# Adding expert results straight into the output, with 71 expert tiles and a rearranged routing stage

## What is computed

```python
h = rmsnorm(layernorm(x), ln1_w)              # then q, k, v, rotary, causal attention, wo
x2 = layernorm(x) + attn @ wo.T
h = rmsnorm(x2, ln2_w).reshape(4096, 256)
topw, topi = top_k(softmax(h @ gate_w.T), 2)  # 8 experts, 2 for each token
topw = topw / topw.sum(-1)
for e in range(8):
    g = silu(h @ w1[e].T) * (h @ w3[e].T)     # 512 wide
    out += (g @ w2[e].T) * wfull[:, e:e + 1]  # 0 where e is not chosen
return x + x2 + out
```

## Time and profile before

| | |
|---|---|
| median of 3 runs | 2072.73 us (2072.46 to 2073.15) |
| the profiled execution | 2073.89 us, span 2072.1 us |
| TensorE busy | 1817.0 us (88%) |
| VectorE busy | 1227.2 us (59%) |
| ScalarE busy | 990.4 us (48%) |
| GpSimd busy | 504.0 us (24%) |
| stage 7 | 1460 to 1616 us |
| stage 8 | 1616 to 2053 us |
| stage 9 | to 2072 us |

### The profile page before, as it was taken

One profiled execution on the slowest core, in us unless ns is written; L12 is line 12 of the kernel. 1 busy time (PEld: TensorE's weight loads), 2 busy tenths in 40 slices (PEclk: granted clock), 3 DMA queues, 4 the chain that ended last, 5 costly groups with the idle time before them and its releaser, 6 DMA issues. The chain is left out here.

```text
span 2072.1 us, 33460 instructions
## 1 busy us (share of the span) xinstructions
PE 1817.0 (88%) x10357; PEld 958.4 (46%) x10358; DVE 1227.2 (59%) x3167; ACT 990.4 (48%) x2129; POOL 504.0 (24%) x740
## 2 busy tenths in 40 slices
PE   5795779884899999999999999999875799999994
PEld 5622656552333333333333333332665466666662
DVE  2388236886888888787888888782466122222220
ACT  2201115431477776767777776867643122222221
POOL 2100302366302030210203030000387122333331
PEclk9997899985899999999999999999986899999997
DMA  4000000000000000000000000000356222222223
GB/s 134 0 0 0 1 1 1 4 18 0 1 2 2 1 2 2 2 1 2 2 2 2 2 2 2 2 1 1 114 170 220 57 47 47 47 47 47 45 47 97
DMA packets 55929, 60.83 MB, mean 29 GB/s; under 512 B 11533, under 2 KB 51638, under 8 KB 55734
## 3 DMA queue, kind: packets, MB, share of 16 engines
q1 hardware_dynamic: 33712, 33.86, 5.5%
q0 software_dynamic: 13440, 18.36, 5.2%
q10 hardware_dynamic: 8646, 6.96, 1.0%
HBM read 34.82 MB, written 28.12 MB: 30 GB/s over the span
## 5 line engine op out<-in xcount | busy, mean ns | idle before, releaser
L1452 ACT ACTIVATE prob<-pS 128x512 f32<-128x512 f32 (+3 forms) x1280 | 600.3, 536 | 245.9 <-PE pS L1366 126.3
L1495 DVE TENSOR_REDUCE mx<-pM 128x1 f32<-128x512 f32 x768 | 501.2, 685 | 92.6 <-PE pM L1346 89.4
L1346 PE MATMUL pM<-KT,QT 96*128 96x512 bf16 (+3 forms) x1280 | 440.9, 356 | 11.7 <-ACT QT L1434 7.3
L1362 PE MATMUL pS<-QT,KT 99*128 99x512 bf16 (+3 forms) x1280 | 416.5, 350 | 14.5 <-ACT prob L1452 9.1
L1381 PE MATMUL pO<-prob,VV 128*32 128x512 f32 (+3 forms) x2560 | 300.6, 542 | 14.2 <-ACT prob L1452 14.0
L1491 DVE CUSTOM_DVE_ANT_0 junk<-pM,mask_row 128x128 bf16<-128x128 f32 (+3 forms) x512 | 243.6, 485 | 71.9 <-PE pM L1346 70.7
L2115 PE MATMUL pH<-w13T,QKV 128*128 x576 | 260.6, 595 | 1.7 <-ACT QKV L2161 1.7
L1346 PEld LDWEIGHTS pM<-KT,QT 96*128 96x128 bf16 x1280 | 124.0, 98 | 263.3 <-DVE mx L1495 99.6
L2203 DVE COPY QKV<-pG 128x512 f32<-128x512 f32 x72 | 49.8, 692 | 317.1 <-PE pG L2124 317.1
L1362 PEld LDWEIGHTS pS<-QT,KT 99*128 99x128 bf16 x1280 | 123.6, 98 | 148.8 <-ACT prob L1452 81.8
L1289 POOL CAST mpart<-mneg 128x16 bf16<-128x16 f32 x32 | 6.8, 213 | 749.6 <-DVE mneg L1503 749.6
(11 more groups left out here) (312 smaller groups left out, 2374.9 us busy)
## 6 DMA issues: line engine op xcount, KB each, us to landing
raw<-in_ffn_w_dram SPq DMA_DIRECT2D x48, 256.0 KB
QKV<-queue SPq DMA_DIRECT2D x72, 136.0 KB, 2.1
x<-_attn_hidden_states_dram SPq DMA_DIRECT2D x32, 128.0 KB, 2.2
acc<-x ACTq DMA_DIRECT2D x8, 512.0 KB
QT<-mrow SPq DMA_DIRECT2D x128, 3.0 KB
queue<-pad_rec SPq DMA_DIRECT2D x9, 136.0 KB
acc<-QKV POOLq DMA_INDIRECT x72
wc_s<-in_attn_Wc_dram ACTq DMA_DIRECT2D x1, 1024.0 KB
```

Of the source, the lines that this page charges most:

```text
L1346: last = nc.tensor.matmul(pM[:, bank, 0:w], QT[0:ROWS, par, h, qt * P:(qt + 1) * P], KT[0:ROWS, par, 512 * part:512 * part + w], start=Tru ...
L1362: last = nc.tensor.matmul(pS[:, p % NSC, lo:512], KT[0:ROWS + 3, par, kt * P:(kt + 1) * P], QT[0:ROWS + 3, par, h, 512 * c + lo:512 * c + ...
L1452: nc.scalar.activation(prob[:, n % 3, h, lo:512], pS[:, p % NSC, lo:512], ACT.Exp, scale=SCALE).then_inc(s.head_exp, 1)
L1495: nc.vector.reduce_max(mx[:, h, qt, part:part + 1], pM[:, plan.bank[item], 0:w], AX.X).then_inc(s.unit_max, 1)
```

## The change

1. Stage 9 and `acc` go. The residual rows are written to the output itself in stage 7, and stage 8's puts add into the output.
2. The output has no rows behind its last token, so padding rows name real tokens, and hold zeros. Two rows of one put may not name the same token. Among the first 128 tokens, a token that is not expert e's is taken for the padding of e: one-hot matrices on VectorE (`spare_hot`, beat 2) and eight small matmuls on TensorE (`spare_tokens`, beat 3) list them; an expert with 128 tokens or more names tokens 0 to 127 in order. ScalarE zeroes a tile of 8 x 272 columns in beat 9.
3. `MAXT` is 71.
4. The eight padding writes are shared by SyncE (even experts) and ScalarE (odd ones). The zero tile at the queue's end is written in beat 2.
5. The residual sum goes from GpSimd to VectorE, at the end of a beat. The first norm's reciprocal roots and negative means are made for all 32 tiles at once by GpSimd in stage 6, after k = 2; `root1` and `negative_mean` go.
6. GpSimd takes `root2` between its two halves of scatters. ScalarE takes the exponential after `h_out` and the first quarter of `weights_out`.
7. Weight block 18 and the ones after it change PSUM banks, because one bank holds the spare tokens for a while.

```diff
-MAXT = 2 * B * L // P + E
+MAXT = 2 * B * L // P + E - 1
@@ stage6, GpSimd
+                def residual_norm():
+                    eps, rstd, shift = (v.norm1[:, n, :] for n in range(3))
+                    nc.gpsimd.tensor_scalar(eps, v.mv5[:, :, 1], 1e-5, None, ALU.add).then_inc(s.norm1, 1)
+                    nc.gpsimd.tensor_scalar(shift, v.mv5[:, :, 0], -1.0, None, ALU.mult).then_inc(s.norm1, 1)
+                    pool.wait_ge(s.norm1, 2)
+                    nc.gpsimd.tensor_tensor(rstd, eps, u.halfpow[:, :].to_broadcast([P, T]), ALU.pow).then_inc(s.norm1, 1)
+                    pool.wait_ge(s.norm1, 3)
+                    nc.gpsimd.tensor_tensor(shift, shift, rstd, ALU.mult).then_inc(s.norm1, 1)
+                    pool.wait_ge(s.norm1, 4)
...
+                    if k == 2:
+                        residual_norm()
@@ stage7, SyncE
                 for beat in range(LATE):
+                    if beat == 2:
+                        sp.wait_ge(s.pad_in, 1)
+                        sp.dma_start(v.queue[E * CAP:E * CAP + P, :], pad).then_inc(s.trash_in, 16)
                     for n in weights_in(beat):
                         raw_load(n)
-                sp.wait_ge(s.pads_known, 1)
-                for e in range(E):
+                sp.wait_ge(s.pads_known, 2)
+                for e in range(0, E, 2):
                     row = sp.value_load(v.pad_at[0:1, e:e + 1], min_val=0, max_val=E * CAP)
-                    sp.dma_start(v.queue[bass.ds(row, P), :], pad[:, :]).then_inc(s.padded, 16)
+                    sp.dma_start(v.queue[bass.ds(row, P), :], padr[:, e, :]).then_inc(s.padded, 16)
@@ GpSimd
                 for beat in range(1, LATE):
                     if beat >= 3:
                         scatter(beat - 3, 0, 4)
-                    if beat + 1 < NQ:
-                        root1(beat + 1)
+                    if beat <= NQ:
+                        root2(beat - 1)
                     if beat >= 3:
                         scatter(beat - 3, 4, 4)
-                    if beat <= NQ:
-                        root2(beat - 1)
-                        residual(beat - 1)
@@ TensorE
+                def spare_tokens():
+                    pe.wait_ge(s.pad_hot, E)
+                    pe.wait_ge(s.wT_out, CUT - RP + 1)
+                    for e in range(E):
+                        last = nc.tensor.matmul(pW[:, CUT % RP, e:e + 1], spare[:, e, :], self_f[:, :], start=True, stop=True)
+                    last.then_inc(s.pad_mm, 1)
@@ ScalarE
+                    if beat == NQ + 1:
+                        act.wait_ge(s.proj, T)
+                        act.wait_ge(s.logits, T // 2)
+                        nc.scalar.activation(turned[:, :], ones[:, 0:1].to_broadcast([P, E * REC]), ACT.Copy,
+                                             scale=0.0).then_inc(s.pad_zero, 1)
                     for j in range(2):
                         if beat < NQ:
                             attended_out(2 * beat + j)
-                        if j == 0 and 2 <= beat <= NQ + 1:
-                            exponential(beat - 2)
                         if 1 <= beat <= NQ:
                             h_out(2 * (beat - 1) + j)
                         weights_out(ws[j * quarter:(j + 1) * quarter])
+                        if j == 0 and 2 <= beat <= NQ + 1:
+                            exponential(beat - 2)
...
+                act.wait_ge(s.pads_known, 2)
+                for e in range(1, E, 2):
+                    row = act.value_load(v.pad_at[0:1, e:e + 1], min_val=0, max_val=E * CAP)
+                    act.dma_start(v.queue[bass.ds(row, P), :], padr[:, e, :]).then_inc(s.padded, 16)
@@ VectorE
+                def residual(q):
+                    four = slice(G * q, G * q + G)
+                    dve.wait_ge(s.x2, G * q + G)
+                    nc.vector.tensor_tensor(x1[:, four, :], x1[:, four, :], QKV[:, four, 0:H], ALU.add).then_inc(s.resid, 1)
...
+                def spare_hot():
...
+                    for e in range(E):
+                        nc.vector.tensor_scalar(spare[:, e, :], column, absent[:, 1, e:e + 1], absent[:, 0, e:e + 1],
+                                                ALU.is_equal, ALU.mult).then_inc(s.pad_hot, 1)
...
                     if 2 <= beat <= NQ + 1:
                         settle(beat - 2)
+                    if beat == 2:
+                        spare_hot()
+                    if beat < NQ:
+                        residual(beat)
@@ stage8
-                with eng.Fori(0, MAXT // R - 1) as i:
+                with eng.Fori(0, (LAST - 2) // R) as i:
...
-                            out=v.acc[:, :], out_offset=bass.IndirectOffsetOnAxis(ap=tail[:, k, E:E + 1], axis=0),
+                            out=v.out_rows[:, :], out_offset=bass.IndirectOffsetOnAxis(ap=tail[:, k, E:E + 1], axis=0),
@@ stage9
-            sp.dma_start(out_rows, acc_rows).then_inc(put, 16)
-            sp.wait_ge(put, 16)
```

More of the change, by code:

```diff
@@ L856, in stages_layer2 @@
         mv5 = sb("mv5", [P, T, 2], F32, late)
+        norm1 = sb("norm1", [P, 3, T], F32, late)
         jrow_i = sb("jrow_i", [P, NTAB], I32, late)
@@ L863, in stages_layer2 @@
         queue = nc.dram_tensor("queue", [E * CAP + P, REC], F32).ap()
-        acc = nc.dram_tensor("acc", [B * L + P, H], F32).ap()
+        out_rows = v.out.rearrange("b l h -> (b l) h")
         with ExitStack() as att:
@@ L1565, in stage7 @@
         junk = sb("junk7", [P, 2, H], BF16, ctx)
-        aT = sb("aT7", [P, 2, 2, C, P], F32, ctx)
-        hT = sb("hT7", [P, 2, 2, C, P], F32, ctx)
+        turned = sb("turned7", [P, E * REC], F32, ctx)
+        aT, hT = (turned[:, 4 * C * P * n:4 * C * P * (n + 1)].rearrange("p (i j c n) -> p i j c n", i=2, j=2, c=C)
+                  for n in range(2))
+        padr = turned[:, :].rearrange("p (e w) -> p e w", e=E)
         ln2c = sb("ln2c", [P, C], F32, ctx)
@@ L1574, in stage7 @@
         iota8 = sb("iota8", [P, E], F32, ctx)
+        self_i = sb("self_i7", [P, 1], I32, ctx)
+        self_f = sb("self_f7", [P, 1], F32, ctx)
+        absent = sb("absent7", [P, 3, E], F32, ctx)
+        early = w2T[:, :, :].rearrange("p f n -> p (f n)")
+        spare = early[:, 0:E * P].rearrange("p (e n) -> p e n", e=E)
+        column = early[:, E * P:E * P + P]
+        pad = early[:, E * P + 2 * P:E * P + 2 * P + REC]
+        column_i = early[:, E * P + P:E * P + 2 * P].bitcast(I32)
         cmp = xl[:, :, :].rearrange("p g h -> p (g h)")[:, 0:E * NTAB].rearrange("p (e j) -> p e j", e=E)
@@ L1792, in _ @@
                     turn_weights(ws[3 * quarter:])
+                    if beat == 3:
+                        spare_tokens()
             @block.scalar
             def _(act):
-                acc_rows = v.acc[0:B * L, :].rearrange("(t p) h -> p t h", p=P)
+                token_rows = v.out_rows.rearrange("(t p) h -> p t h", p=P)
                 def attended_out(i):
@@ L1962, in _ @@
                                             ALU.mult).then_inc(s.gw_ready, 1)
-                negative_mean(0)
-                negative_mean(1)
                 for beat in range(LATE):
@@ L1969, in _ @@
                         choose(beat - 2)
+                    if beat == 4:
+                        spare_out()
                     if beat < NQ:
                         attended(beat)
-                    if 1 <= beat and beat + 1 < NQ:
-                        negative_mean(beat + 1)
                     if 2 <= beat <= NQ + 1:
                         settle(beat - 2)
+                    if beat == 2:
+                        spare_hot()
+                    if beat < NQ:
+                        residual(beat)
                 dve.wait_ge(s.total, 1)
@@ L2072, in _ @@
                             load(R * i + k + R, k)
+                    for j in range(MAXT // R * R, MAXT):
+                        sp.wait_ge(s.x_T, j - R + 1)
+                        sp.wait_ge(s.tail_in, j - R + 1)
+                        load(j, j % R)
                 @block.gpsimd
@@ L2095, in _ @@
                             keep(k, i + 1)
-                    for j in range(MAXT - R + 1, MAXT):
+                    for j in range(MAXT // R * R - R + 1, MAXT):
                         put(j, j % R)
+                        if j + R - 1 >= MAXT // R * R and j + R - 1 < MAXT:
+                            keep((j + R - 1) % R, (j + R - 1) // R)
                     pool.wait_ge(y_put, 16 * MAXT)
@@ L2212, in _ @@
                     steps(dve, step)
-def stage9(nc, sb, ps, sem, env, base_env):
-    v, u = Names(env), base_env
-    put = sem("f_put")
-    with nc.Block() as block:
-        @block.sync
-        def _(sp):
-            out_rows = u.out.rearrange("b l h -> (b l h)").rearrange("(a n) -> a n", a=P)
-            acc_rows = v.acc[0:B * L, :].rearrange("l h -> (l h)").rearrange("(a n) -> a n", a=P)
-            sp.dma_start(out_rows, acc_rows).then_inc(put, 16)
-            sp.wait_ge(put, 16)
```

93 lines of the change are left out of this document (48 added, 45 removed).

## The result

The changed kernel took 2035.02 us (median, 2034.13 to 2035.73); the kernel before, timed beside it, 2072.6 (2069.19 to 2073.15). The ratio is 0.982, with an interval of 0.981 to 0.984: 33 to 40 us faster. The forecast was 2027.6, 7.4 us too fast. Its direction and its range (2016 to 2042) held; the narrower stretch of 2022 to 2034, to which it gave most weight, did not, nor did the size of the gain: 45.1 us were forecast, 37.6 lie between the medians.

What follows compares the result with a forecast made beforehand. GpSimd was taken to bound stage 7's beats 3 to 7, SyncE's padding its end, TensorE the expert tiles. Copy 18.0, tile 5.8 and stage 7 21.3 sum to 45.1 us off 2072.73: 2027.6, range 2016 to 2042.

Steps and rivals of the forecast that it cites:

- That closing: End of the kernel, after the last put's landing: closing the block was taken as 1.0 us, making the copy's gain 18.0.
- what is late next is this pair: End of stage 7: padding and scatters end together, so stage 8 starts at 1595 instead of 1616.3, gaining 21.3 us.
- Last scatter's end 1593.0: Stage 7, GpSimd: 1608.1 - 19.8 - 2.1 + 1.2 + 2.6 + 3.0 = 1593.0 us.
- The wait for squares: Stage 7: root2, between the scatter halves, waits once on GpSimd for ScalarE's squares, about 2.6 us.
- The stalls beside the residual: Stage 7: VectorE's residual stalls GpSimd six times, 0.2 us each, costing 1.2 (0 to 7).
- The "remote" waits: Stage 7: VectorE's waits for something on none of its engines reach GpSimd more, costing 3 us (0 to 8).
- rival 3: Stage 7, the port: each VectorE residual stops a scatter for 1.2 us and delays root2; 6 us more, 2033; chance 0.05.
- Rival 2: Stage 7: another engine or the DMAs become the bound; gain only 5 to 14 us, time 2035 to 2044; chance 0.22.
- Rival 4: Stage 8's puts: accumulating into the output costs more, or padding rows collide; slower, 2120 at 2.5 us more; chance 0.03.
- Rival 1: Stage 7 gives all: no remote wait felt, squares ready; scatters end 1586, gain 28, time 2021 (2016 to 2022); chance 0.15.
- 5: Rival: end waits as long without the copy, stage 7's beat stays 15.5 us; only the tile gains, 2067; chance 0.03.
- terms taken as nothing: Effects priced at zero, among them stage 6's power of 32 columns on GpSimd (1.04 to 8.3 us) and ScalarE's zeroing.

## Why the prediction was right, and where its size was off

Its own three terms, in the span: the copy 15.1 for 18.0, the tile 5.1 for 5.8, stage 7 18.1 for 21.3. The missing 6.8 us are these steps.

1. *"That closing ... at least nothing, and at most the 3.8 us ... I take 1.0."* It is 3.9 (2030.0 to 2033.9), 3.4 of it GpSimd's drain. The bound was right, the choice wrong: the guess that most of the gap was the start of the next block was never looked up, although the sequencers' rows of before had the drain of 3489 ns. The runs with the copy and without the drains show it. Mis-sized by 2.9 us.

2. *Padding "ends about when the scatters do, and what is late next is this pair. Stage 8 starts at 1595".* Two errors and one omission. The writes took 1.13 us, not 2.14, and were done 10 us before the last scatter's end. What is late next is the scatters alone, and from their end to the first load of stage 8 are 7.9 us: the landing (1.7), the drain (5.3) and the meeting of the engines with the clearing of semaphores (0.9), where the prediction had 2. That cost 6 us. That the padding ended stage 7 was a reading of a single execution; the kernel before with the padding on two queues (ratio 1.000) and without the drains (9.0 us faster, eight writes in 9.4 us) show that the drain bound it in the executions that were timed; in the profiled one the two ended within 0.2 us. Moving the padding is worth nothing, in either kernel. The drain of stage 7 is the term that the forecast did not have at all.

3. *Last scatter's end 1593.0.* It was 1590.3. Term by term: the work taken from GpSimd, 19.8, is right (14.0 and 5.8 in the group rows of before). "2.1 earlier" for the first scatter: 35.0 us after SyncE's first transfer of the stage (in three of the four traces of before and its variants, 33.0 in the other) became 32.1, so 2.9, of which the run with the residual on GpSimd gives 2.1 to the residual. The wait for squares, 2.6: 2.38, once, as foreseen. The stalls beside the residual, 1.2 (0 to 7): 4.9, four times what was taken. The "remote" waits, 3.0: none. So two errors of 3.7 and 3.0 us hid each other, and 2.6 us of the 112.9 were such waits as well: from the chain's usual 110.3 us, 110.3 - 19.8 + 2.4 + 4.9 = 97.8, and measured were 97.9. That 1593.0 lay within 2.7 us of the measured end was luck.

4. *The tile.* 5.8 in the run with 72 tiles. The stage's difference of 5.1 in one pair of profiles is inside what single executions differ by.

So rival 3's mechanism held (its time was 2033), and its 1.2 us for each of six residuals was nearer (7.2 in all, measured 4.9) than the forecast's 0.2. The one small row on which the prediction took 0.2 was a scatter that began 0.37 us after a shorter operation; it showed the tail of a stall and not its size. The page "SBUF — State Buffer" of the Trainium skill, section "SBUF: two separate sides", says that the other engine is shut out for the whole operation, and the traces agree in nearly full size: the scatter of 2.01 us lost 1.05 while 1.16 us of the residual were left. But that section tells the starving of GpSimd's transfers only of VectorE's two-port modes, a condition that the prediction left out. The same page's section "Who interferes with whom" reports that a `tensor_tensor` had not been seen to stall a transfer, and infers that making descriptors needs only the write side of the port pair, while such an operation takes the read side; here a scatter or a small operation of GpSimd's was held up beside each residual, and the measurement decides. Rival 2 gives the measured time (2035 to 2044) but not its cause: no beat was bound by another engine. Rival 4 is out (a put of 3.81 us against 3.75), and so are 1 and 5. Rival 1's 1586 does not follow from its two conditions: 1593.0 less 3.0 and 2.6 is 1587.4. Of the terms taken as nothing, two can be read: the power of 32 columns took 5.4 us of GpSimd's idle time in stage 6, and the zeroing on ScalarE 2.0 us, and the chain of scatters shows neither.

What stays open: why the drain takes 5285 ns at the end of stage 7 and 3407 to 3489 at that of stage 8, and what it does in that time; and what held back the padding writes and two of VectorE's operations in the profiled execution of before. Whether the other executions of before that were timed then had it too can't be said, as only one has a trace. If none had, the change in stage 7 is worth 15.3 us (from SyncE's first transfer in stage 7 to its first in stage 8 are 153.95 us in the kernel before with the padding on two queues, 138.63 in after), and the sum is 15.1 + 5.8 + 15.3 = 36.2. Between the medians timed together are 37.6 us, and 35.9 from the kernel before's 2070.9, its median in the group with most runs of it (13).

## What to carry to other kernels

Before a stage's end is put down to a transfer, look at what every engine's sequencer does there: the closing of a block had a price of 3.4 to 5.3 us that no busy time and no chain of waits showed, and it alone was worth more than the order of root2 and the padding on two queues together. A step that is late last in one execution may not be in the next; eight writes that took 17.1 us in one trace took 8.8 and 9.4 in others, so a row that ends a stage by a few tenths should be held against a second trace and against the engine next in line. A cost that is left out at one place should be looked for at the next: stage 8's drain came back in stage 9's block. And a VectorE operation with two inputs in SBUF beside a GpSimd that is the bound costs it up to most of its own length there (0.4 to 1.05 us of 1.22), though moving the work was still worth 10 us.

## What the runs showed of the hardware

- GpSimd's drain after a stage of indirect transfers took 5285 ns (64 scatters) in all ten traces of stage 7 that have it, whether it began 1.7 or 5.8 us after the last scatter, and 3407 or 3489 ns after 71 or 72 puts, so 82 ns more for the one put more. In the blocks where GpSimd had issued no transfers it took 41 to 1051 ns in after, as in this one:

```profile
L1230 POOLq DRAIN  x1: 299/299/299, 1413.5 to 1413.5; - x1
```

with one exception, where its sequencer came to the drain while eight additions of 18.7 us were still under way:

```profile
L427 POOLq DRAIN  x1: 18791/18791/18791, 229.4 to 229.4; - x1
```
```profile
229.41 18.69 POOL L436 TENSOR_TENSOR base<-base,bo_b 128x1024 f32<-128x1024 f32 x8 [21.58 <-PE pX L449]
```

At the ends of stages 7 and 8 nothing of the kind was under way: the last transfer had landed.

- Left out behind the wait for all transfers, the two drains (8.7 us) gave back 7.3 us in the changed kernel and 9.0 in the one before. In the latter the drain of 3489 ns stood in the next block instead, beside a transfer that took longer.
- A scatter whose issue begins 0.05 us after a residual of 1.21 us on VectorE takes 2.01 us, one beside none 0.96; the power of four columns 1.89 and 1.04. A residual that began 0.63 us after a scatter took 1.22 us all the same, and the scatter behind it 1.41.
- A put that adds into the output took as long to its landing as one into another tensor: 3.81 and 3.75 us.
